# History attention of a Perceiver stack: the deviation spread by transposes, the squares transposed and summed along the row by VectorE

## What is computed

```python
eh = _gelu(_ln(historical_data @ hist_W + hist_b, hist_ln_g, hist_ln_b))   # 12544 x 512
aw = _gelu(eh @ ctx_W1 + ctx_b1) @ ctx_W2 + ctx_b2
aw = softmax(aw, axis=1)
cc = sum(eh * aw, axis=1)
# _ln: (x - mean) * rsqrt(mean((x - mean)^2) + 1e-5) * g + b, over the 512 features of a row
```

## Time and profile before

| | us |
|---|---|
| median of 3 runs | 991.49 (990.98 to 992.1) |
| span of the profiled execution, first to last instruction | 987.2 |
| of it, from the first `mean_square` to the last | 23.4 to 399.0 |
| TensorE busy over the span | 833.1 (84%) |
| VectorE, ScalarE, GpSimd busy | 642.5, 532.3, 106.4 |

### The profile page before, as it was taken

How to read it: one execution, slowest core, us unless ns; L and a number is a source line. 1 busy time by engine, 2 the same in 40 slices (tenths; PEclk the granted TensorE clock), 3 DMA queues, 4 the chain that set the end, 5 groups by cost and what they waited for, 6 DMA issues and landing times. The chain is left out here.

```text
span 987.2 us, 20927 instructions
## 1 busy us (share of the span) xinstructions
PE 833.1 (84%) x8380; PEld 665.3 (67%) x8380; DVE 642.5 (65%) x1323; ACT 532.3 (54%) x896; POOL 106.4 (11%) x116
## 2 busy tenths in 40 slices
PE   3999999999999999772275956999999999998756
PEld 3988878878888788451143932677777777776544
DVE  3555657776667676889814359798998889921151
ACT  2777787776867777822101100576776667784010
POOL 1332222222222222000000000000000000000010
PEclk9999999999999999976555985699999999999576
DMA  3366535644555354292057079389989978360000
GB/s 118 123 156 169 150 112 142 184 125 151 148 154 151 119 145 121 66 264 91 0 89 112 1 162 175 63 161 193 201 198 159 199 182 160 96 212 5 0 1 5
DMA packets 83089, 124.94 MB, mean 127 GB/s; under 512 B 10728, under 2 KB 73450, under 8 KB 82220
## 3 DMA queue, kind: packets, MB, share of 16 engines
q1 hardware_dynamic: 82992, 123.61, 52.0%
HBM read 84.06 MB, written 39.52 MB: 125 GB/s over the span
## 5 line engine op out<-in xcount | busy, mean ns | idle before, releaser
L1707 DVE TENSOR_REDUCE unit_max<-bank 128x1 f32<-128x512 f32 (+1 forms) x350 | 221.3, 675 | 31.4 <-PE bank L911 29.1
L1241 ACT ACTIVATE prob<-bank 128x1024 f32<-128x1024 f32 (+1 forms) x200 | 191.0, 1005 | 82.0 <-PE bank L935 81.4
L630 PE MATMUL bank<-hc_high,w_high 128*128 128x256 f32 x392 | 117.5, 300 | 8.6 <-POOL hc_low L1294 8.4
L911 PE MATMUL bank<-k_stack,q_max 49*128 49x512 f32 (+1 forms) x400 | 107.4, 535 | 18.6 <-DVE unit_max L1703 11.4
L1391 DVE SCALAR_TENSOR_TENSOR normed<-bank,b_centered,rstd_wide 128x256 f32<-128x256 f32 x196 | 85.4, 478 | 48.0 <-ACT rstd_wide L1106 47.9
L950 PE MATMUL bank<-prob,vals 128*32 128x128 f32 x3136 | 111.5, 283 | 3.3 <-issue 3.3
L935 PEld LDWEIGHTS bank<-q_stack,k_stack 49*128 49x128 f32 x1568 | 105.9, 193 | 11.1 <-ACT q_stack L1233 2.7
L630 PE MATMUL bank<-hc_high,w_low 128*128 128x256 f32 x392 | 112.6, 287 | 0.0
L630 PE MATMUL bank<-hc_low,w_high 128*128 128x256 f32 x392 | 112.2, 286 | 0.0
L935 PE MATMUL bank<-q_stack,k_stack 49*128 49x128 f32 x1568 | 105.8, 273 | 2.2 <-ACT prob L1241 0.9
L950 PEld LDWEIGHTS bank<-prob,vals 128*32 128x32 f32 x3136 | 82.5, 112 | 26.1 <-issue 22.2
(11 more groups left out here) (302 smaller groups left out, 1268.5 us busy)
## 6 DMA issues: line engine op xcount, KB each, us to landing
k_stack<-k_scratch SPq DMA_DIRECT2D x336, 112.0 KB, 5.4
vals<-v_scratch SPq DMA_DIRECT2D x8, 1666.0 KB, 8.4
v_scratch<-vst SPq DMA_DIRECT2D x12, 1088.0 KB, 9.6
hc_raw<-in_ctx_t SPq DMA_DIRECT2D x49, 256.0 KB, 3.1
k_scratch<-k_high SPq DMA_DIRECT2D x49, 256.0 KB, 3.4
k_scratch<-k_low SPq DMA_DIRECT2D x49, 256.0 KB, 3.5
w_ffn<-in_l SPq DMA_DIRECT2D x4, 1920.0 KB, 13.2
w_l<-in_l SPq DMA_DIRECT2D x6, 603.0 KB, 5.7
```

The costliest lines, as they stand in the source:

```text
L630: last = nc.tensor.matmul(out_ap, lhs, rhs, start=(n == 0), stop=(n == len(pairs) - 1))
L911: last = nc.tensor.matmul(bank[:, at, 0:hi - lo], q_max[head_rows[hh], s, :], k_stack[s % 2][head_rows[hh], lo:hi], start=True, stop=True)
L1241: A(prob[:, e % NPB, :, 0:width], bank[:, at:at + 2, 0:width], ACT.Exp).then_inc(c_exp, 1)
L1707: V.tensor_reduce(unit_max[:, s % 2, u, hh:hh + 1], bank[:, at[hh], 0:width], AX_X, ALU.max, negate=True).then_inc(c_red, 1)
```

## The change

The same places in every engine's order hold the same number of instructions as before. `mean_square` and `spread_rstd` call a transpose in place of a float32 product, with the same stationary operands; `mean_square` now writes 256 columns of bank 4 instead of 2. `variance` sums these along the row, 128 numbers for each of its two results, in place of adding epsilon to two numbers. Epsilon goes into `add_squares`, whose second instruction gets a scalar added to its sum, and the factor 1/512 of the mean goes into the scale of `widen`.

```diff
             def mean_square(n):
...
                 for s in range(2):
-                    last = nc.tensor.matmul(bank[:, 4, CH + s:CH + s + 1], square1[:, s * HB:(s + 1) * HB],
-                                            inv_width[:, 0:1], start=True, stop=True)
+                    last = nc.tensor.transpose(bank[:, 4, CH + s * HB:CH + (s + 1) * HB],
+                                               square1[:, s * HB:(s + 1) * HB], ident)
                 last.then_inc(h_ms, 1)
             def spread_rstd(n):
...
                 for s in range(2):
-                    last = nc.tensor.matmul(bank[:, 4, s * HB:(s + 1) * HB], h_rstd[:, s:s + 1].broadcast_to([P, P]),
-                                            ident, start=True, stop=True)
+                    last = nc.tensor.transpose(bank[:, 4, s * HB:(s + 1) * HB], h_rstd[:, s:s + 1].broadcast_to([P, P]),
+                                               ident)
                 last.then_inc(h_bc, 1)
             def widen(n):
...
-                A(rstd_wide[:, :], bank[:, 4, 0:CH], ACT.Copy).then_inc(h_rw, 1)
+                A(rstd_wide[:, :], bank[:, 4, 0:CH], ACT.Copy, scale=float(C2) ** 0.5).then_inc(h_rw, 1)
             def variance(n):
...
-                V.tensor_scalar(h_var[:, :], bank[:, 4, CH:CH + 2], LN_EPS, None, ALU.add).then_inc(h_ve, 1)
+                V.tensor_reduce(h_var[:, :], bank[:, 4, CH:2 * CH].rearrange("p (s c) -> p s c", s=2), AX_X,
+                                ALU.add).then_inc(h_ve, 1)
             def add_squares(n):
...
-                V.tensor_tensor(square1[:, :], square2[:, 0, :], square2[:, 1, :], ALU.add).then_inc(h_add1, 1)
+                V.scalar_tensor_tensor(out=square1[:, :], in0=square2[:, 0, :], scalar=C2 * LN_EPS / P,
+                                       in1=square2[:, 1, :], op0=ALU.add, op1=ALU.add).then_inc(h_add1, 1)
```

## The result

The changed kernel took 979.75 us (median of 6 runs, 977.52 to 981.91). The kernel before, run beside it, took 999.15 (6 runs, 990.98 to 1017.38). Two later comparisons of the unchanged pair gave 0.9821 (0.9757 to 0.9885) and 0.9831 (0.9765 to 0.9897). So the change is worth 1.2 to 1.8%, 12 to 18 us. The forecast was 979 and faster. The time lies beside the one foretold, but by luck: the loop gained a third more than the working gave it, the stages behind it did not simply move with its end, and the two errors offset each other. Most of what follows is about them.

What follows compares the result with a forecast made beforehand. TensorE was taken to bound the loop: 30 plain turns at 0.33 give 9.9 us, stalls 2.0, last group 0.6, first turns -0.1, total 12.4; 991.5 less this is 979 us, range 974.5 to 985.5.

Steps and rivals of the forecast that it cites:

- The price of a transpose: TensorE in the chunk loop: 0.118 us per transpose, entry included, so a plain turn shrinks by 0.33 us, bounds 0.08 to 0.43.
- What follows the loop hangs on its end and moves with it: Stages behind the chunk loop: the loop's saving of 12.4 us passes unchanged to the end of the kernel.
- What bounds the loop: Middle of the chunk loop: TensorE, busy 48.18 of 50 us, sets the pace before and after the change.
- the chain: Path from `keys_full` over VectorE's `variance` and `deviation` to the spread's load; slack falls from 0.50 to 0.11 us per plain turn.
- VectorE: In each turn `variance` rises from 0.152 to 0.424 us (+0.27, on the path to `deviation`), `add_squares` by 0.06.
- turns 1 to 4: Loop's start: turns 1 and 2 lengthen by 0.13 us each (VectorE leads), 3 and 4 by 0.07 (ScalarE's first Gelu leads).
- The stalls: Four places in the loop where TensorE waits 1.9 us at `values_turn` for late ScalarE; 0.56 us saved around each.
- One fall fewer: Rival at the loop's stalls: one or two clock falls more or fewer, 1.3 to 2.6 us either way; no separate chance.
- The baseline: Whole kernel: saving taken off the 991.49 us median; the profiled span of 987.2 us lies 4.3 under it.
- The chain takes over: Rival in plain turns: the reduction costs 0.68 us, a turn gives only 0.18, total 986 us; chance 0.09.
- The transposes save nothing: Rival on TensorE: two transposes after a float32r matmul cost as much as four replaced records; 993.8 us, slower; chance 0.05.
- The clock falls more often: Rival in the loop: transposes not counting as activity bring more falls, 1.3 us each; 999 us; chance 0.04.

## Where the prediction failed, and where it held

Two steps failed. The price of a transpose was set too high (0.118 us taken, 0.109 measured), so a plain turn gave 0.41 us and not 0.33, and the loop 16.4 and not 12.4. And the loop's gain was handed on to the end as it was: "What follows the loop hangs on its end and moves with it". In the first pair of profiles the stages behind the loop gave 5.7 us of it back, in the second they added 1.3. That 979.75 lies beside 979 is luck.

**What bounds the loop: right.** TensorE set the pace before and does after. The forecast was a slack of 0.11 for the chain; 0.08 to 0.10 was measured, of which 0.05 passes even when the load waits, and the run with the sum made twice shows that the chain is that close.

**The price of a transpose: too high.** The step took 0.118, with all of the entry into the transposes in it, and had 0.105, from the stalled group, as the lowest price. It measured 0.11 both in the row of six and in the spread. The squares gave 0.17, not 0.12, the spread 0.22 by the rows and 0.24 in the turn, not 0.20. A turn gave 0.41, not 0.33; the bound of 0.43 was nearly reached. The mistake was to choose the row with a mixed neighbour in it and to spread its entry over all transposes. Taken one by one, the four transposes of the kernel before start 0.142, 0.109 and 0.110 apart: only the first, behind the products with one column, is dear. In the kernel after all six start 0.108 to 0.110 apart, so behind a float32r matmul that entry is not paid. The lower bound of a turn was also worked out wrongly: if all of the 0.59 were the transposes', the group before cost 0.36 + 0.59 = 0.95 and the six 0.89, which saves 0.06 and does not lose it, so the bound is 0.20 and not 0.08.

**VectorE: right for one, wrong for the other.** `variance` took 0.418 (forecast 0.424). `add_squares` stayed at 0.425, where I added 0.06 from another three-operand form; so turns 1 to 4 gained about 0.02 each instead of losing 0.13 and 0.07.

**The stalls: the mechanism was right.** Four of 2.2 us, forecast four of about 2. At equal clock the stalled turn kept its 10.33, the turn ahead gave 0.09 and the turn behind 0.41: 0.50 against the 0.56 of the forecast. The other two stalled turns, at the lower clock, shrank by 0.1 to 0.2. One fall fewer gave 1.3, which the forecast had as a rival within its range. The number of falls is a draw too: six profiles with this loop have two, two, two, one, none and none, and the loop took 358.9, 359.0, 358.8, 357.6, 356.5 and 356.5 us from first to last `mean_square`; the three profiles with the loop of before have three falls each. The loop's sum: 30 plain turns by 0.405 are 12.2, the stalls with the turns around them 2.3, the fall 1.3, turns 0 to 4 and the last 0.6: 16.4, and 16.1 by the trace (0.2 of it because the loop's first `mean_square` starts 0.2 later), against 12.4.

**"What follows the loop hangs on its end and moves with it": this step failed.** It was true for the order of the work and false for its duration. I had looked at the granted clock only where the change is, and took the low clock from 589.8 to 634.2 in the profile of before as part of the kernel; it is one draw. In the first profile after, the same stretch ran to 644.9 and took 6 us back, in the second to 617.9. Between three profiles of the kernel after, the stretch from the first exponential to the last differs by 17 us (276.4, 285.8 and 293.6), more than the error of any term in the loop, and this term belonged into the range.

**The baseline.** The sum stood on 991.49, a median of three runs that agreed within 1.1 us, and took the 4.3 us between it and the span for time outside the instructions. In every execution for which both are on record the span lies only 1.7 to 2.3 us under the time, so the profiled execution was itself one of about 989 us (an estimate from these). With 33 more runs of the same kernel the four comparisons have medians of 994.5 to 999.15, and single runs reach 1039.14. By the first pair of profiles the span fell 10.4, by the second 18.1. So a loop gain some 4 us larger than forecast and a loss in the cross attention, set against a low baseline, made 979.75, beside 979. The working was right in the loop's mechanism, too small in its size, and blind behind it.

**The rivals.** *The chain takes over*: no, the reduction cost 0.418 and not 0.68. *The transposes save nothing*: no, the first transpose behind a float32r matmul starts 231.66 - 231.54 = 0.12 after it, as its neighbours do. *The clock falls more often*: not by transposes. The Trainium skill, page "TensorE: Matmul & The Clock Gate", section "Part 4: PE-mode transpose", says that transposes do not count as activity for the clock the way matmuls do. With eight of them in a turn the plain turns of this trace ran at 1.00, and there were fewer falls in the loop, two instead of three, so no run here shows that they cost the clock anything when they stand among matmuls. The low clock that mattered lay in the cross attention, whose instructions the change leaves as they were.

## What to carry to other kernels

A float32 product with the identity can be a transpose, which takes half the records at the same price for each; that price is best read inside a run of equal records, not at its edge. Before a saving in one stage is handed on to the end, look at the granted clock in the stages behind it: if a stretch there lasts differently in two profiles of the same kernel, that difference is a term of the sum with its own bounds. To measure a change in one stage, compare in the traces how long that stage takes from its own first instruction to its last; here that agreed to 0.1 us between profiles with the same number of falls, where its end moved by 0.8 and medians by 10 to 20. And a change that makes the code longer or shorter moves where instruction blocks end in everything behind it: a padded kernel with the same work shows whether that matters.

## What the runs showed of the hardware

Three things were unexpected. First, TensorE's clock stayed at 0.50 for up to 75 us (569.8 to 644.9) although in the last 40 of them TensorE was busy 98%, with products of 49 rows and of 32 columns of weights. Second, in the cross attention TensorE stood for 0.3 us or more without waiting for any engine only at the ends of blocks of 256 of its instructions, up to 3.3 us; at the standing of 2.23 us the data queue filled the DMA engines meanwhile. Each of the ten low stretches of 6.8 to 41 us that began behind the first exponential began within 2 us of the end of such a standing; the other 18 standings of 0.6 us or more were followed by no long one.

Third, GpSimd held VectorE up: with the loop's new phase `low_part` (228.09 to 229.37) runs beside `add_squares`' first instruction (228.65 to 229.92), whose median went from 0.748 to 1.257 us. Without overlap it takes 0.68; with 0.2 us of overlap it took 0.75 in the kernel before, with 0.72 it takes 1.27, while `low_part` keeps its 1.27. `normalise`, ahead of it, was not slower beside the same `low_part`. Plain turns show no price for it: they became shorter by what TensorE saved.
